# GpSimd's indirect DMAs in groups of five, each group behind the landing of the last

## The reference

```python
h = jnp.maximum(_layernorm(x), 0.0)                       # layer 0
msgs = (h * node_vec1)[src]                               # gather by source
x = x + segment_sum(msgs, dst, 12500) * node_vec1_n2      # sum by destination
h = jnp.maximum(_layernorm(x), 0.0)                       # layer 1
m = relu(h[src] + edge_attr_32)                           # gather, add the edge's row
x = x + (1.0 + eps) * h + segment_sum(m, dst, 12500)
```

## Time and profile before

| | us |
|---|---|
| median of the three runs | 4981.2 |
| lowest, highest | 4978.56, 4985.58 |
| profiled execution: its span, from the first instruction to the last | 8580.9 |
| in it: TensorE busy | 4359.2 (51%) |
| in it: VectorE busy | 3658.4 (43%) |
| in it: GpSimd busy | 3610.0 (42%) |
| in it: ScalarE busy | 3124.7 (36%) |

### The profile page before, as it was taken

How to read it: one execution, slowest core, us unless ns; L and a number is a source line. 1 busy time by engine, 2 the same in 40 slices (tenths; PEclk the granted TensorE clock), 3 DMA queues, 4 the chain that set the end, 5 groups by cost and what they waited for, 6 DMA issues and landing times.

```text
span 8580.9 us, 129759 instructions
## 1 busy us (share of the span) xinstructions
PE 4359.2 (51%) x44428; PEld 3164.9 (37%) x44428; DVE 3658.4 (43%) x11303; ACT 3124.7 (36%) x8299; POOL 3610.0 (42%) x3712
## 2 busy tenths in 40 slices
PE   0555555555555555555555555445444444545444
PEld 0333333333333333333333333334334343434343
DVE  6444444444444444444444444434343333434334
ACT  0333434343333333333333333234333333433333
POOL 7444444444444444444444444343443434343442
PEclk8777777777777777777777777666666666666666
DMA  5111111111111111111111100101110111101110
GB/s 90 31 31 31 31 31 31 31 30 31 30 31 30 31 30 31 30 31 30 31 30 31 31 17 17 43 22 31 30 32 22 32 29 32 31 22 32 30 32 17
DMA packets 437255, 265.45 MB, mean 31 GB/s; under 512 B 330740, under 2 KB 421220, under 8 KB 430120
## 3 DMA queue, kind: packets, MB, share of 16 engines
q1 hardware_dynamic: 318264, 185.91, 9.1%
q0 software_dynamic: 116960, 65.42, 4.4%
q10 hardware_dynamic: 1296, 4.79, 0.2%
HBM read 176.35 MB, written 79.52 MB: 30 GB/s over the span
## 4 chain that ended last, share of the span: by engine, by line
PE 36%; issue 26%; another core or an unknown queue 22%; DVE 9%; ACT 5%; SPq 1%; DVEq 0%; ACTq 0%; DMA 0%; POOL 0%; POOLq 0%
PE candidates L1179 16%; DVE arena L1663 5%; PE candidates L1105 5%; PE plain_ps L1191 4%; PE sorted_agg L1122 4%; DVE arena L1639 3%; PE key_rows L1074 2%; ACT centered L974 2%; PE candidates L1100 2%; ACT message L920 2%; PE plain_ps L1143 1%; PE candidates L1092 1%; ACT arena L821 1%; PE plain_ps L1151 1%
## 5 line engine op out<-in xcount | busy, mean ns | idle before, releaser
L710 POOL DMA_INDIRECT records<-stage,place_i x1875 | 1821.1, 971 | 675.8 <-issue 625.1
L698 POOL DMA_INDIRECT stage<-table,src_plain x1250 | 1193.9, 955 | 1778.1 <-DMA stage<-in_edge_attr 1386.7
L1639 DVE TENSOR_SCALAR arena<-arena,row_key 125x1280 bf16<-125x1280 f16 x1000 | 552.6, 553 | 2554.9 <-ACT arena L821 1776.0
L920 ACT ACTIVATE message<-candidates,member_is 128x96 bf16<-128x96 f32 x3600 | 912.4, 352 | 1643.5 <-remote 922.8
L691 POOL DMA_INDIRECT message<-table,mid_src x480 | 533.5, 1112 | 2234.8 <-PE plain_ps L1151 2095.5
L1105 PE MATMUL candidates<-parts,arena 125*128 125x32 bf16 x15000 | 589.2, 181 | 1214.2 <-issue 1211.8
L821 ACT ACTIVATE arena<-key_rows 125x640 f16<-125x640 f16 x1000 | 662.5, 719 | 1237.3 <-remote 987.2
L1663 DVE TENSOR_SCALAR arena<-window_iota,dst_rel 128x224 bf16<-128x224 f16 (+1 forms) x4800 | 1025.9, 280 | 112.4 <-remote 67.7
L1105 PEld LDWEIGHTS candidates<-parts,arena 125*128 125x128 bf16 x15000 | 503.7, 99 | 1384.6 <-issue 1370.1
L1092 PE MATMUL candidates<-parts,arena 125*128 125x96 bf16 x5000 | 312.0, 220 | 1312.9 <-ACT message L920 748.6
L1074 PE MATMUL key_rows<-ident,record 128*125 128x128 f16 x5000 | 494.6, 242 | 878.4 <-issue 587.7
(11 more groups left out here) (224 smaller groups left out, 5798.9 us busy)
## 6 DMA issues: line engine op xcount, KB each, us to landing
record<-records SPq DMA_DIRECT2D x50, 1650.0 KB, 7.1
stage<-in_edge_attr SPq DMA_DIRECT2D x125, 400.0 KB, 3.2
records<-pad SPq DMA_DIRECT2D x25, 1650.0 KB, 10.7
records<-stage,place_i POOLq DMA_INDIRECT x1875
stage<-table,src_plain POOLq DMA_INDIRECT x1250
message<-table,mid_src POOLq DMA_INDIRECT x480
xs<-in_x SPq DMA_DIRECT2D x8, 390.6 KB
table<-parts ACTq DMA_DIRECT2D x4, 585.9 KB
```

Source lines behind the costliest of these rows:

```text
L698: pool.indirect_dma_start(message[:, k, j, :] if l == 0 else rows[:, k, j, :], None, table0 if l == 0 else table1, bass.IndirectOffsetOnAx ...
L710: pool.indirect_dma_start(records, bass.IndirectOffsetOnAxis(ap=place_i[:, h, e:e + 1], axis=0), stage[:, h, e, :], None).then_inc(scatter ...
L920: last = nc.scalar.activation(direct_message[n % DB][:, m * WIDE:(m + 1) * WIDE], candidates[n % 2][:, m * WIDE:(m + 1) * WIDE], ACT.Copy, ...
L1639: nc.vector.tensor_scalar(src_onehot[:, g % 2, o, :], key_row[:, g % 2, :], row_key[0:NP, o:o + 1], None, ALU.is_equal).then_inc(src_oneho ...
```

## The change

In `gather_mid`, in `gather` for layer 1 and in `scatter`, GpSimd waits before each fifth indirect DMA (`j` or `e` = 5, 10, ...) until all DMAs of the run so far have landed, on the semaphore that they raise anyway. That makes 14 waits in a scatter of 75, 3 in a middle gather of 20 and 4 in a gather of 25. The last batch of layer 0 and the loops for stray edges, which call `gather` without `before`, get none. `gather_mid` has the batch as a further argument for the value that it waits for.

```diff
+            RUN = 5
+
-            def gather_mid(h):
+            def gather_mid(b, h):
                 pool.sem_inc(gathers_begun, 1)
                 for j in range(MID):
+                    if j % RUN == 0 and j > 0:
+                        pool.wait_ge(gathered[0][0], 16 * MID * b + 16 * j)
+                        pool.sem_inc(gathers_begun, 1)
                     pool.indirect_dma_start(
...
-            def gather(l, k, tiles, landed, indices):
+            def gather(l, k, tiles, landed, indices, before=None):
                 pool.sem_inc(gathers_begun, 1)
                 for j in tiles:
+                    if before is not None and j % RUN == 0 and j > 0:
+                        pool.wait_ge(landed, before + 16 * j)
+                        pool.sem_inc(gathers_begun, 1)
                     pool.indirect_dma_start(
...
                     if is_first(b) and e % J == 0:
                         pool.wait_ge(first_ranked, e // J + 1)
+                    if e % RUN == 0 and e > 0:
+                        pool.wait_ge(scattered[h], 16 * SE * (u - 1) + 16 * e)
+                        pool.sem_inc(scatters_begun, 1)
                     pool.indirect_dma_start(
...
-                    gather_mid(h)
+                    gather_mid(b, h)
...
-                    gather(1, k, range(J), gathered[1][k], src_plain[:, k, 0:J])
+                    gather(1, k, range(J), gathered[1][k], src_plain[:, k, 0:J], 16 * J * b)
```

## The result

The changed kernel takes **6424.2 us** (median of four runs, 6406.95 to 6426.12) against 4979.9 us of the kernel before, measured beside it (4976.27 to 4985.58): a ratio of 1.289, 95% interval 1.287 to 1.291. That is 1444 us more. The direction was forecast; the amount, 1042 us, was too small, and the time lies above the range.

The account below looks back on a forecast made before the run. GpSimd's chain of indirect DMAs was taken as the bound; 350 scatter waits at 1.5 us (525) plus 272 gather waits at 1.9 (517) add 1042 to the median 4981.2, giving 6023 us, range 5807 to 6256, widened to 5790 to 6270.

Parts of the forecast that it names:

- GpSimd's chain is the ordinary execution: Whole kernel: GpSimd's indirect DMAs with their gaps set the ordinary time, about 4995 us, despite its waits in the profile.
- The agreement of 4995 with the median: Whole kernel: 4740.9 us of DMAs and gaps, 210.3 around them and 44 for restarts, 0.3% from the median of 4981.2.
- Every wait is exposed: Scatters, middle gathers, layer 1: nothing hides the 622 added waits, since GpSimd has no slack; 1042 us together.
- the gap that belongs to the profile: Rival, all GpSimd DMAs: the 0.30 us gaps exist only under profiling, so time stays at 4980 us; chance 0.06.
- the one layer with slack: Rival, layer 0 or layer 1: one layer hides its waits, giving 5361 or 5643 us; chance 0.08.
- the rival in which waits pass at once: Rival, all added waits: they are already met when reached and do not hold GpSimd; chance under 0.01.
- the landing of a gather, "1.2": Middle gathers and layer 1: landing 1.2 us after the DMA's end, making 1.9 us a wait, 517 for 272.
- The rival of landings under load: Rival, all added waits: loads delay landings to 2.0 us, so each wait costs 2.7 us, giving 6660 us; chance 0.08.
- A scatter's wait: Layer 0 scatters: landing 0.82 plus restart 1.0 less gap 0.30, 1.5 us each, 525 for 350 waits.
- the 91 kept as a bound: Middle gathers: pauses might give back 0.19 us on each of 480 DMAs, 91 us, counted only in the lower end.
- the signs: Changed kernel's profile: fives at the old spacing, gaps of 1.8 and 2.2 us, runs of 116 and 39 us.
- The profiled span: Whole profile of the changed kernel: its span should rise by less than the median, since slow stretches hide waits.

Follow-up runs that it names:

- the run with met waits: The changed kernel with all 622 waits kept, but each on a semaphore met long ago instead of a landing; 4986.6 us, ratio 0.9999 to the kernel before.
- By part, alone: Three kernels, each the changed kernel with only one part's waits: scatter 5590.6 us, middle gather 5364.6, layer 1 5473.1, against 4985.0 for the kernel before.

## Why the prediction was right and wrong

**GpSimd's chain is the ordinary execution: right.** It was read against a profile that showed GpSimd waiting for others, and the run with met waits shows it directly: 4848 of 4986 us. The agreement of 4995 with the median was luckier than it looked, though. Undisturbed, the DMAs and gaps take 4848 us and not 4741 (scatters start about 1.35 us apart, (1963.7 + 570.9) / 1875, where the sum had 1.30, and layer 1's DMAs 1.31, where it had 1.25), and everything around them about 138 and not 254. Among the 254 were 44 us for runs that start behind a wait; in the run with met waits they follow the run before after 0.30 us. Two errors canceled.

**Every wait is exposed: right.** The parts add up, and the rows of waits give the time. The two rivals on hiding, the gap that belongs to the profile and the one layer with slack, fall with that (the gaps of 0.30 us stand in the profile that isn't stretched too); so does the rival in which waits pass at once.

**The step that failed is the landing of a gather, "1.2", in the term of 1.9 us each, 517 together.** By itself the quiet price was nearly right: quiet gaps are 2.00 us for scatters and 2.15 for gathers, so 350 x 1.70 + 272 x 1.85 = 1098 us against 1042. The 346 us on top are landings that took longer than quiet ones. By part, alone: scatter 606 against 525, middle gather 380 against 137, layer 1 488 against 380; the middle gather is 243 of the miss. Above the quiet price lie 11 us in the scatter, 247 in the middle gather and 118 in layer 1. Of the 247, 192 are shown to come from the stage loads and the fill; the other 55 are put down to the record load without a run that shows it. Of the 118, 84 are shown to come from the record load; some 30 stay open.

**Why the rows misled.** The landing was read at 2778.36 us, in a middle gather that had waited 93.19 us for TensorE, more than 60 us after SyncE had sent that batch's loads (from 2702.65 to 2715.75 us in that trace). But the prediction had just argued that this wait doesn't exist in an ordinary execution. Without it the gather begins where the scatter ends, which is exactly where SyncE's queue begins. The duration was taken from an undisturbed place, as one should; the place wasn't one that the ordinary execution has.

**The rival of landings under load had the mechanism and the wrong shape.** It took its rows from the loads of the start, which was the right sign, but priced all 622 waits at 2.7 us or none, and got 8 in 100. The loads strike where they run: two in three waits of a middle gather are long; of layer 1's 200 waits 25 last over 4 us; of the scatters' 350 only two have packets of SyncE's beside them. Priced by place it would have belonged into the forecast, not beside it.

**Smaller terms.** A scatter's wait was 0.82 + 1.0 - 0.30; it is 1.19 + 0.81 - 0.30. The restart is a little shorter, and the landing longer than the last packet shows, because the semaphore comes after it: the packets of a quiet scatter are through 0.80 us after its end, as the prediction read it, and the semaphore rises 0.39 us later. The prediction set the rows against the Trainium skill (DMA: Bandwidth & Descriptors, Anatomy of one DMA - SWDGE (gpsimd) path), which has a fixed cost of about 2.0 us, most of it the receipt, heaviest towards HBM. The 2.2 us from issue to landing of a scatter agree with the size. The order doesn't show in the whole landing, 1.19 us into HBM and 2.15 - 0.79 = 1.36 into SBUF. It shows only between the last packet and the semaphore, 0.39 us for a quiet scatter and 0.29 for a quiet gather, and that is not most of 2 us. The pauses gave next to nothing back: a scatter DMA is 1027 ns long in the changed kernel against 1047 with met waits, 1875 x 0.02 = 38 us, less than the 91 kept as a bound. The 0.19 us behind that bound belonged to the stretched trace: with met waits, middle DMAs start 1.28 us apart and layer 1's 1.31. The runs came out longer than the signs named, too: in the median 123.7 us for a scatter of 75 (116 forecast) and 42.3 for a gather of 25 in layer 1 (39 forecast).

**The profiled span** was to rise by less than the median. It fell, from 8580.9 to 6423.7 us, because the stretch is gone; the step assumed that any profile of this kernel has it, and none of the other runs does.

## What to carry to other kernels

A wait for a transfer's landing turns a cost that nobody saw, because the queue ran on, into one that each wait pays: here a stop and restart of 0.5 us and a landing of over 1 us even in the quiet. Price it at the place where it will stand in the ordinary order of work, and ask what the other queues send in just those microseconds; here the landing that let them go was that of the very scatter behind which the gather starts. And when a profile is found to be stretched, its gaps are gone and its neighbours with them: don't take a duration from a place that the same argument has done away with.

## What was not expected of the hardware

- GpSimd's issuing didn't notice the busy DMA queues here: with SyncE's transfers beside it, its DMAs kept coming every 1.25 us, while their packets lagged by at least 87. Only the landing was delayed: a wait for it grows from 2.2 us to as much as 10.5.
- A stop of GpSimd between two indirect DMAs takes 0.8 us from the descriptors' end to the next start, 0.5 more than the ordinary gap, the same in all three places and beside SyncE's loads too. A met wait cost nothing that could be measured.
- Even without SyncE's transfers about a fifth of layer 1's waits are 0.4 to 1.9 us longer than quiet ones, all of them beside packets of the instruction queues. Not settled.
- Only the profile of the kernel before was stretched. What did that wasn't tried.
